# Batch 1 of a mixer-and-FFN kernel: rows split in SBUF and transposed by the DMA queue instead of by TensorE

## What is computed

```python
x = x + layernorm(attn(layernorm(x)))
x = x + layernorm(ffn(layernorm(x)))

# attn: i, f, g = x @ Wi.T, x @ Wf.T, x @ Wg.T          (512 x 512 weights)
gate = sigmoid(f);  v = silu(i) * (1 - gate)
_, o = associative_scan(combine, (gate, v), axis=1)     # o[t] = gate[t]*o[t-1] + v[t]
o = o * rsqrt(mean(o*o) + EPS) * gnorm_w * g * sigmoid(g);  return o @ Wo

# ffn: hidden = silu(x @ W1.T) * (x @ W3.T)             (hidden width 2048)
hidden = fwht(hidden);  return hidden @ W2.T
```

## Time and profile before

| | |
|---|---|
| median of 3 runs | 684.47 us (682.37 to 684.54) |
| the profiled execution | 685.5 us, its span 683.7 us |
| PE busy | 659.0 us, 96% |
| DVE busy | 413.2 us, 60% |
| ACT busy | 352.6 us, 52% |
| POOL busy | 237.7 us, 35% |
| DMA | 114.12 MB, mean 167 GB/s |

### The profile page before, as it was taken

One profiled execution on the slowest core, in us unless ns is written; L12 is line 12 of the kernel. 1 busy time (PEld: TensorE's weight loads), 2 busy tenths in 40 slices (PEclk: granted clock), 3 DMA queues, 4 the chain that ended last, 5 costly groups with the idle time before them and its releaser, 6 DMA issues. The chain is left out here.

```text
span 683.7 us, 11532 instructions
## 1 busy us (share of the span) xinstructions
PE 659.0 (96%) x4332; PEld 427.1 (62%) x4332; DVE 413.2 (60%) x791; ACT 352.6 (52%) x633; POOL 237.7 (35%) x216
## 2 busy tenths in 40 slices
PE   4998999999999899999999999999999999999996
PEld 2444444444456667776776777677777777777762
DVE  5889999999999999976459203144212113621224
ACT  5999886373674767645346334344333343533231
POOL 1328368574762145165227112112211111411121
PEclk9999999999999999999999999999999999999999
DMA  8992453107245465984796225568334233752002
GB/s 324 408 403 101 108 140 59 46 21 170 92 157 184 169 202 191 319 291 171 177 308 238 110 108 178 106 199 289 137 131 165 83 133 108 243 204 81 29 1 92
DMA packets 60743, 114.12 MB, mean 167 GB/s; under 512 B 40464, under 2 KB 40720, under 8 KB 56080
## 3 DMA queue, kind: packets, MB, share of 16 engines
q1 hardware_dynamic: 60688, 113.39, 49.8%
HBM read 80.87 MB, written 23.07 MB: 152 GB/s over the span
## 5 line engine op out<-in xcount | busy, mean ns | idle before, releaser
L646 PE MATMUL ps<-xb,ring 128*128 128x256 f16 (+1 forms) x696 | 209.5, 301 | 5.5 <-ACT ps L990 3.0
L648 PE MATMUL ps<-xb,ring 128*128 128x256 f16 (+1 forms) x696 | 209.4, 301 | 0.0
L647 PE MATMUL ps<-xb,ring 128*128 128x256 f16 (+1 forms) x696 | 209.4, 301 | 0.0
L1451 POOL TENSOR_TENSOR ring<-sga,ring 128x512 f16<-128x512 f32 x64 | 80.1, 1256 | 289.5 <-ACT ring L1036 289.4
L646 PE MATMUL ps<-ring 128*128 128x256 f16 x384 | 104.8, 273 | 0.0
L647 PE MATMUL ps<-ring 128*128 128x256 f16 x384 | 104.7, 273 | 0.0
L648 PE MATMUL ps<-ring 128*128 128x256 f16 x384 | 104.7, 273 | 0.0
L646 PE MATMUL ps<-w2t,ring 128*128 128x512 f16 x256 | 97.1, 379 | 1.1 <-ACT ring L921 1.1
L647 PE MATMUL ps<-w2t,ring 128*128 128x512 f16 x256 | 97.1, 379 | 0.0
L648 PE MATMUL ps<-w2t,ring 128*128 128x512 f16 x256 | 97.1, 379 | 0.0
L646 PEld LDWEIGHTS ps<-xb,ring 128*128 128x128 f16 x696 | 68.1, 98 | 43.0 <-ACT ps L990 5.2
(11 more groups left out here) (169 smaller groups left out, 1053.1 us busy)
## 6 DMA issues: line engine op xcount, KB each, us to landing
ring<-w_comb SPq DMA_DIRECT2D x24, 1792.0 KB, 7.5
...
```

The source lines that it names most:

```text
L646: pe.matmul(dst, a_hi, b_hi, start=start, stop=False, skip_group_check=onto)
L647: pe.matmul(dst, a_hi, b_lo, start=False, stop=False, skip_group_check=onto)
L648: return pe.matmul(dst, a_lo, b_hi, start=False, stop=stop, skip_group_check=onto)
L1451: pool.tensor_tensor(hid(b, c, 1), sga[:, c % 2], hid(b, c, 0), ALU.subtract).then_inc(hid_lo, 1)
```

## The change

`AHEAD` goes from 2 to 1, so batch 1 takes the second form: `XT.1.0` to `XT.1.3` leave TensorE's order, `XD.1.0` to `XD.1.3` enter SP's, and ACT and DVE do `XT.1.*` from `rows` in SBUF into `sga` and `hsp`. Since batch 2 uses the same two buffers, `XT.2.*` on ACT now waits for batch 1's DMA transposes. `XL.2.t` waits for `XT.1.t`'s low part on DVE instead of for TensorE's transpose. All five tables are new (banks too).

```diff
-AHEAD = 2
+AHEAD = 1
...
                 elif b > 1:
-                    sp.wait_ge(xt_mm if b == 2 else xt_lo, TC * (b - 1) + t + 1)
+                    sp.wait_ge(xt_lo, TC * (b - 1) + t + 1)
                 sp.dma_start(rows[:, t], x_rows[TC * b + t]).then_inc(ld_x[t], 16)
...
             def transpose_x(b, t):
                 sp.wait_ge(xt_lo, TC * b + t + 1)
-                if t == 0:
+                if t == 0 and b > 1:
                     for read in (f_mm, i_mm, g_mm):
                         sp.wait_ge(read, KC * (b - 1))
...
                     act.wait_ge(aw_norm, 3)
-                    if b == 3:
-                        act.wait_ge(ld_xt, 16 * TC)
+                    if b > AHEAD:
+                        act.wait_ge(ld_xt, 16 * TC * (b - AHEAD))
                     act.activation(parts_of_x(t)[:, 0], rows[:, t], ACT.Copy).then_inc(xt_hi, 1)
```

The places of the tables that the prediction speaks of:

```diff
 PE:   (banks left out)
-... AN.3.0 XT.1.0 F.0.2 XT.1.1 F.0.3 I.0.0 I.0.1 I.0.2 XT.1.2 G.0.0 G.0.1 G.0.2 I.0.3 G.0.3 XT.1.3 H2.0.0 H2.0.1 F.1.0
+... AN.3.0 F.0.2 F.0.3 I.0.0 I.0.1 I.0.2 G.0.0 G.0.1 G.0.2 I.0.3 G.0.3 H2.0.0 H2.0.1 F.1.0
 SP:
-... UL.6.0 UL.7.0 XL.2.0 NL.5.0 XL.2.1 NL.6.0 XL.2.2 NL.7.0 XL.2.3 XD.2.0 XL.3.0 ...
+... UL.6.0 UL.7.0 NL.5.0 XL.2.0 XD.1.0 XL.2.1 XL.2.2 NL.6.0 NL.7.0 XD.1.1 XD.1.2 XL.2.3 XD.1.3 XD.2.0 XL.3.0 ...
 POOL:
-... FW.0.5 FW.0.6 X1.2.0 P.0.0 FW.0.7 S.0.1 ...
+... FW.0.5 P.0.0 FW.0.6 FW.0.7 X1.2.0 S.0.1 ...
 DVE:
-... XT.2.0 FD.1.4 MS.0.0 FD.1.5 FD.1.6 FD.1.7 Y.0.0 X1.3.0 FD.2.0 XT.2.1 YN.0.0 XT.2.2 S.1.0 Y.0.1 ...
+... XT.2.0 FD.1.4 FD.1.5 FD.1.6 MS.0.0 FD.1.7 XT.2.1 FD.2.0 X1.3.0 Y.0.0 XT.2.2 S.1.0 YN.0.0 Y.0.1 ...
```

More of the change, by code:

```diff
@@ new lines @@
+F.2.0:4 G.1.3:3 I.2.0:1 G.2.0:2 F.2.1:5 H2.1.0:6 H2.1.1:4 H2.2.0:0 H2.2.1:3 MS.1.0:7 Y.1.0:1 Y.1.1:2 Y.1.2:5 Y.1.3:6
+I.2.1:4 G.2.1:0 F.2.2:3 I.2.2:7 H2.3.0:1 H2.3.1:2 G.2.2:5 F.2.3:6 I.2.3:4 F.3.0:0 G.2.3:3 I.3.0:7 G.3.0:5 MS.2.0:1
+Y.2.0:6 Y.2.1:2 H2.4.0:0 Y.2.2:4 H2.4.1:3 Y.2.3:7 F.3.1:5 I.3.1:1 G.3.1:6 F.3.2:0 H2.5.0:3 H2.5.1:2 I.3.2:5 G.3.2:4
+F.3.3:7 I.3.3:0 GP.0.0:6 G.3.3:1 H2.6.0:3 GP.0.1:7 GQ.0.0:5 GQ.0.1:4 GR.0.0 H2.6.1:2 GR.0.1 MS.3.0:0 Y.3.0:1 Y.3.1:3
+GP.0.2:6 GU.0.0 GU.0.1 H2.7.0:2 GP.0.3:7 Y.3.2:0 H2.7.1:1 GQ.0.2:5 Y.3.3:3 GR.0.2 GQ.0.3:4 GU.0.2 GP.0.4:6 GR.0.3
@@ new lines @@
+D.0.0 GU.0.3 D.0.1 GQ.0.4:5 D.0.2 GR.0.4 GP.0.5:7 D.0.3 D.0.4 D.0.5 D.0.6 D.0.7 GQ.0.5:4 GU.0.4 GR.0.5 D.0.8 GP.0.6:6
+D.0.9 D.0.10 D.0.11 GU.0.5 GP.0.7:7 GQ.0.6:5 D.0.12 D.0.13 D.0.14 D.0.15 GR.0.6 GQ.0.7:4 D.0.16 D.0.17 GR.0.7 GU.0.6
+D.0.18 D.0.19 GU.0.7 GP.0.8:6 D.0.20 D.0.21 GQ.0.8:5 GP.0.9:7 D.0.22 D.0.23 GR.0.8 GQ.0.9:4 D.0.24 D.0.25 D.0.26
+GR.0.9 D.0.27 GP.0.10:6 GU.0.8 D.0.28 D.0.29 GU.0.9 GP.0.11:7 D.0.30 D.0.31 GQ.0.10:5 GQ.0.11:4 GR.0.10 GR.0.11
+GU.0.10 D.0.32 D.0.33 D.0.34 GP.0.12:6 D.0.35 D.0.36 D.0.37 D.0.38 GQ.0.12:5 GU.0.11 D.0.39 GP.0.13:7 GR.0.12
@@ new lines @@
+GQ.0.13:4 GU.0.12 GR.0.13 GP.0.14:6 D.0.40 D.0.41 GU.0.13 D.0.42 D.0.43 D.0.44 D.0.45 GQ.0.14:5 D.0.46 GP.0.15:7
+GR.0.14 GQ.0.15:4 D.0.47 GP.1.0:6 GR.0.15 D.0.48 D.0.49 D.0.50 GU.0.14 D.0.51 D.0.52 D.0.53 GP.1.1:7 D.0.54 GQ.1.0:5
+D.0.55 GU.0.15 GR.1.0 GU.1.0 GP.1.2:6 D.0.56 D.0.57 GQ.1.1:4 D.0.58 GR.1.1 D.0.59 D.0.60 D.0.61 GQ.1.2:5 D.0.62 GU.1.1
+GP.1.3:7 GR.1.2 D.0.63 GU.1.2 GP.1.4:6 D.1.0 GQ.1.3:4 GQ.1.4:5 GR.1.3 D.1.1 D.1.2 D.1.3 GP.1.5:7 GU.1.3 GR.1.4 D.1.4
+D.1.5 GQ.1.5:4 GP.1.6:6 GU.1.4 D.1.6 GR.1.5 D.1.7 GQ.1.6:5 GP.1.7:7 D.1.8 D.1.9 D.1.10 GR.1.6 GU.1.5 D.1.11 D.1.12
@@ new lines @@
+GP.1.8:6 D.1.13 D.1.14 D.1.15 GQ.1.7:4 D.1.16 GR.1.7 D.1.17 GU.1.6 D.1.18 D.1.19 D.1.20 GP.1.9:7 GU.1.7 D.1.21
+GQ.1.8:5 D.1.22 GQ.1.9:4 GR.1.8 GU.1.8 D.1.23 D.1.24 GR.1.9 GP.1.10:6 GP.1.11:7 D.1.25 GQ.1.10:5 D.1.26 GR.1.10 GU.1.9
+GP.1.12:6 GU.1.10 D.1.27 D.1.28 D.1.29 D.1.30 D.1.31 D.1.32 D.1.33 GQ.1.11:4 GQ.1.12:5 GR.1.11 GU.1.11 GR.1.12
+GP.1.13:7 GU.1.12 D.1.34 D.1.35 D.1.36 D.1.37 D.1.38 D.1.39 GQ.1.13:4 D.1.40 GR.1.13 GU.1.13 GP.1.14:6 GP.1.15:7
+GQ.1.14:5 GQ.1.15:4 GR.1.14 D.1.41 GR.1.15 D.1.42 D.1.43 D.1.44 D.1.45 D.1.46 D.1.47 GU.1.14 GU.1.15 D.1.48 GP.2.0:6
@@ new lines @@
+GP.2.1:7 D.1.49 D.1.50 D.1.51 GQ.2.0:5 D.1.52 D.1.53 D.1.54 D.1.55 D.1.56 GR.2.0 D.1.57 D.1.58 D.1.59 GP.2.2:6 GU.2.0
+GQ.2.1:4 D.1.60 D.1.61 GR.2.1 D.1.62 D.1.63 GU.2.1 GQ.2.2:5 GP.2.3:7 GR.2.2 GQ.2.3:4 GU.2.2 GR.2.3 GP.2.4:6 GP.2.5:7
+GU.2.3 GQ.2.4:5 D.2.0 GR.2.4 GQ.2.5:4 D.2.1 GR.2.5 GU.2.4 GP.2.6:6 GU.2.5 D.2.2 GP.2.7:7 GQ.2.6:5 D.2.3 D.2.4 D.2.5
+GQ.2.7:4 D.2.6 GR.2.6 D.2.7 GR.2.7 D.2.8 GU.2.6 D.2.9 GP.2.8:6 D.2.10 GU.2.7 D.2.11 GP.2.9:7 D.2.12 GQ.2.8:5 D.2.13
+GR.2.8 D.2.14 D.2.15 GQ.2.9:4 D.2.16 GU.2.8 D.2.17 GR.2.9 GP.2.10:6 GU.2.9 D.2.18 D.2.19 GQ.2.10:5 GP.2.11:7 GR.2.10
@@ new lines @@
+GQ.2.11:4 GP.2.12:6 D.2.20 D.2.21 D.2.22 D.2.23 D.2.24 D.2.25 GU.2.10 GR.2.11 GU.2.11 GQ.2.12:5 GP.2.13:7 GR.2.12
+GQ.2.13:4 GP.2.14:6 GU.2.12 D.2.26 D.2.27 D.2.28 D.2.29 D.2.30 D.2.31 D.2.32 D.2.33 D.2.34 GQ.2.14:5 D.2.35 D.2.36
+GR.2.13 D.2.37 D.2.38 GP.2.15:7 GR.2.14 D.2.39 GU.2.13 D.2.40 D.2.41 D.2.42 D.2.43 GQ.2.15:4 GP.3.0:6 D.2.44 GU.2.14
+GR.2.15 D.2.45 GU.2.15 GQ.3.0:5 D.2.46 GR.3.0 GU.3.0 GP.3.1:7 D.2.47 GP.3.2:6 GQ.3.1:4 GQ.3.2:5 GR.3.1 D.2.48 D.2.49
+GR.3.2 D.2.50 D.2.51 GU.3.1 GU.3.2 D.2.52 GP.3.3:7 D.2.53 D.2.54 GQ.3.3:4 D.2.55 GP.3.4:6 D.2.56 GR.3.3 D.2.57
@@ new lines @@
+GQ.3.4:5 D.2.58 D.2.59 GR.3.4 D.2.60 GU.3.3 GP.3.5:7 D.2.61 GU.3.4 GQ.3.5:4 D.2.62 D.2.63 D.3.0 D.3.1 GR.3.5 D.3.2
+GP.3.6:6 D.3.3 D.3.4 D.3.5 GU.3.5 GQ.3.6:5 GP.3.7:7 GR.3.6 GQ.3.7:4 D.3.6 GR.3.7 D.3.7 GU.3.6 D.3.8 GU.3.7 D.3.9
+D.3.10 D.3.11 D.3.12 GP.3.8:6 D.3.13 D.3.14 GQ.3.8:5 D.3.15 GR.3.8 D.3.16 GP.3.9:7 D.3.17 GP.3.10:6 GQ.3.9:4 GU.3.8
+GR.3.9 D.3.18 D.3.19 GQ.3.10:5 GP.3.11:7 GR.3.10 D.3.20 D.3.21 GU.3.9 GU.3.10 D.3.22 D.3.23 GP.3.12:6 GQ.3.11:4
+GQ.3.12:5 GR.3.11 GR.3.12 GU.3.11 GP.3.13:7 D.3.24 D.3.25 D.3.26 D.3.27 D.3.28 D.3.29 D.3.30 D.3.31 GQ.3.13:4
@@ L81 @@
+GP.3.14:6 D.3.32 D.3.33 GU.3.12 GR.3.13 D.3.34 GQ.3.14:5 GP.3.15:7 GU.3.13 D.3.35 GR.3.14 D.3.36 GU.3.14 D.3.37 D.3.38
+D.3.39 GQ.3.15:4 D.3.40 GR.3.15 GU.3.15 D.3.41 D.3.42 D.3.43 D.3.44 D.3.45 D.3.46 D.3.47 D.3.48 D.3.52 D.3.56 D.3.60
+D.3.49 D.3.53 D.3.57 D.3.61 D.3.50 D.3.54 D.3.58 D.3.62 D.3.51 D.3.55 D.3.59 D.3.63
 """
@@ L99 @@
[L99 to L103, removed]
+F.3.2 H2.5.0 H2.5.1 S.3.1 I.3.2 P.3.1 G.3.2 S.3.2 F.3.3 WT.4.0 I.3.3 WT.4.1 SH.1.0 P.3.2 GP.0.0 WT.5.0 WT.5.1 G.3.3
@@ new lines @@
+GP.0.1 GQ.0.0 S.3.3 GQ.0.1 P.3.3 H2.6.0 GA.0.0 H2.6.1 UP.0.0 GA.0.1 WT.6.0 GP.0.2 YN.3.0 WT.6.1 WT.7.0 WT.7.1 SH.2.0
+YN.3.1 H2.7.0 GP.0.3 UP.0.1 H2.7.1 GQ.0.2 YN.3.2 GA.0.2 GQ.0.3 GA.0.3 GP.0.4 WT.8.0 WT.8.1 WT.9.0 WT.9.1 GQ.0.4 SH.3.0
+YN.3.3 UP.0.2 ZT.1.0 UP.0.3 ZT.1.1 GP.0.5 GQ.0.5 GA.0.4 GA.0.5 GP.0.6 SH.4.0 UP.0.4 UP.0.5 GP.0.7 WT.10.0 GQ.0.6
+WT.10.1 WT.11.0 WT.11.1 ZT.1.2 GQ.0.7 ZT.1.3 ZT.1.4 ZT.1.5 GA.0.6 GA.0.7 WT.12.0 WT.12.1 GP.0.8 WT.13.0 ZT.1.6 SH.5.0
+UP.0.6 GQ.0.8 UP.0.7 WT.13.1 GP.0.9 GQ.0.9 GA.0.8 GA.0.9 SH.6.0 UP.0.8 UP.0.9 GP.0.10 GP.0.11 WT.14.0 GQ.0.10 WT.14.1
@@ L122 @@
[L122 to L125 removed]
+X1.2.1 S.0.2 X2.2.0 P.0.2 FD.1.0 XT.1.3 FD.1.1 S.0.3 X1.2.2 P.0.3 X1.2.3 X2.2.1 FD.1.2 X2.2.2 X2.2.3 FD.1.3 XT.2.0
@@ new lines @@
+GU.0.10 WT.15.0 GR.0.11 WT.15.1 GU.0.11 SA.7.0 UP.0.10 SO.7.0 UP.0.11 Z1.2.0 GR.0.12 Z1.2.1 Z1.2.2 GU.0.12 GR.0.13
+GU.0.13 UP.0.12 Z1.2.3 Z2.2.0 Z2.2.1 Z2.2.2 Z2.2.3 ZT.2.0 UP.0.13 ZT.2.1 ZT.2.2 GR.0.14 GU.0.14 ZT.2.3 ZT.2.4 ZT.2.5
+GR.0.15 GU.0.15 ZT.2.6 UP.0.14 UP.0.15 GR.1.0 GU.1.0 GR.1.1 GU.1.1 UP.1.0 V.0.0 V.0.1 W.0.0 V.0.2 UP.1.1 W.0.1 GR.1.2
+GU.1.2 V.0.3 W.0.2 GR.1.3 GU.1.3 UP.1.2 W.0.3 UP.1.3 Z1.3.0 GR.1.4 Z1.3.1 GU.1.4 Z2.3.0 Z2.3.1 Z1.3.2 ZT.3.0 ZT.3.1
+Z2.3.2 GR.1.5 GU.1.5 UP.1.4 Z1.3.3 Z2.3.3 ZT.3.2 GR.1.6 ZT.3.3 GU.1.6 ZT.3.4 UP.1.5 ZT.3.5 ZT.3.6 GR.1.7 GU.1.7 UP.1.6
```

163 lines of the change are left out of this document (59 added, 104 removed).

## The result

The changed kernel takes 689.23 us (median of 4 runs, 688.71 to 690.01) against 683.85 for the kernel before beside it: ratio 1.0083, 95% interval 1.006 to 1.0105. The forecast was 687.4 us, slower. The profiled execution took 688.79 us, span 687.0. Single executions of the same early orders also begin up to 1.7 us apart, so of a start only differences above that mean something.

A forecast was written before the change was run, and what follows sets the result against it. Bound: PE and DVE both full from 60 to 285 us (221.0 and 217.6 of 225), then PE alone. Sum: 685.5 + 2.9 = 688.4, and 687.4 us as the runs' median lies 1.0 below the profiled execution; range 683.0 to 690.0.

The forecast's parts named there:

- 1.7 us off TensorE are worth 0: Ahead of H2.0.0: four transposes leave PE, 1.7 us, but become idle time since F.1.0 is not ready; gain 0.
- F.1.0 at 63.5, +3.9: Start of batch 1: F.1.0 waits for the last DMA transpose, XD.1.3, and starts 3.9 us later (3.4 to 5.3).
- No slack: ACT from 28 to 58 us: busy 29.78 of 30.00 us, so it can't reach XT.1.3 earlier than 58.23 us.
- The queue, 0: DMA queue before F.1.0: dry at 59.4 us, just before XD.1.3 is issued; 0, at most 2 us more.
- The clock, +2.1: After PE's 5.7 us idle before F.1.0: PE restarts at 1.2 GHz, costing 2.1 us (0 to 2.6).
- DVE, +2.8 behind XT.2.1: DVE near 72 to 77 us: three steps now come behind XT.2.1, 2.8 us of work left (0 to 3.5).
- F.1.1 at 84.7 without a wait: PE at F.1.1: Y.0.3 ends 6.0 us late at 84.7, no wait for S.1.0; 5.0 us behind the old 79.77.
- Back to 2.9 at 285 us, then carried: PE up to 285 us: lateness shrinks from 5.0 to about DVE's 2.8, taken as 2.9, then carried to the end.
- Rival 1: 60 to 285 us: DVE's 2.8 us do not reach PE, lateness is absorbed; 684.5 us, up to 686.4; chance 0.28.
- five places: 60 to 285 us: PE waits on DVE and ACT at only five places, 3.9 us in all; argument for Rival 1.
- The later tables, 0, at most 1.5 to lose: From 285 us on: new orders change neighbours of about the same steps; 0, with 2.4 us to gain, 1.5 to lose.
- the cushion: PE's waits up to 285 us, which in Rival 1 absorb its lateness: 3.9 - 3.9 = 0.

The follow-up runs named there:

- e10: Changed kernel with SP's and DVE's border orders of before, plus early steps moved on ACT, DVE, SP and POOL for an earlier F.1.0 and fewer DVE waits; 683.8 us.
- e12: e10 with one more step moved: P.2.3 ahead of ZT.0.6 in DVE's order; 682.8 us.
- e11: e2 with SP's and DVE's border steps as in the kernel before; 687.0 us.
- e2: Kernel before, its transposes unchanged, with the changed kernel's late orders on all five engines (PE from D.0.0 on); 689.0 us.
- e4: Changed kernel with 12 matmuls of no use ahead of H2.0.0 and 26 ahead of F.1.0 to keep TensorE busy; 688.8 us.
- e8: Changed kernel with the late orders of before, and XT.1.3 (ACT, DVE) and XD.1.1 to XD.1.3 (SP) moved earlier; 690.1 us.
- e6: Changed kernel with SP's seventeen steps at the border near 362 us in the order of the kernel before; 686.6 us.

## Why the prediction came out, step by step

- **1.7 us off TensorE are worth 0.** Right: PE waits 2.85 us at H2.0.0 and 5.75 at F.1.0. That they would be worth something with F.1.0 free fits e10 and e12, but no run isolates it: these two differ from the kernel before in much else.
- **F.1.0 at 63.5, +3.9.** Measured 62.27, +2.64. The mechanism is right, the term was too large because ACT reached XT.1.3 at 56.52 and not at 58.2. Most of that is the late execution of before: in e11 and e2, with the early orders of before, ACT gets there at 57.20 and 57.26 us, and in the kernels with the new early part that leave XT.1.3 in its place between 55.82 and 57.34. "No slack" held, but it said nothing of where ACT's list starts. Against e11 F.1.0 is 3.66 late, close to the forecast. SP issued XD.1.3 at 58.60, 0.4 us behind XL.2.3 as forecast; to F.1.0 it took 3.7 us, forecast 3.6.
- **The queue, 0.** Right at this place, but the transposes cost SP time: see below.
- **The clock, +2.1.** Measured 1.7 (9.49 against 7.77 us from F.1.0 to MS.0.0; e4). It fell already in H2.0.0, which took 2.39 in place of 1.96 us. The Trainium skill (TensorE: Matmul & The Clock Gate, "What's actually happening") calls the throttled state the default; the trace now agrees inside the kernel, at 0.50. But removing the fall gives 0.4 us at the end (e4), within the spread of the runs: its price was hidden, and what hid it is in the next point.
- **DVE, +2.8 behind XT.2.1.** The wait came (1.43) and DVE lost 2.4 us between the scans at 60.5 and 79.8, but more of it through X1.2.3's root (1.71 us of idle time), a chain over ACT and POOL that I hadn't followed. And Y.2.0 came between 163.2 and 164.2 us in every kernel with the new early orders but e10 and e12, wherever F.1.1 was (82.0 to 84.2 us). Where F.1.1 came at 82.9 us or later the wait in front of Y.2.0 was 0.3 to 0.8 us, where it came earlier (e4, e8) 1.7 and 2.4: there DVE's place for P.2.3 is the second stop. No step of the forecast named it.
- **F.1.1 at 84.7 without a wait.** Measured 82.92, without a wait. It is 1.8 us less late than forecast, 1.3 from F.1.0's start and 0.4 from the clock. Against e11's 78.75 it is 4.2 late, where the forecast had 5.0.
- **Back to 2.9 at 285 us, then carried.** The waits shrank from 2.96 to 0.96 us up to 285 us, so 1.15 was left there and not 2.9; one wait of 0.21 at 302 us makes it 1.35 at 345. About 1.0 of the missing 1.75 is again the late execution of before. (Rival 1's "five places" where PE waits on DVE and ACT are four on ACT and one of 0.31 us on issue; PE waits for DVE nowhere there before.)
- **The later tables, 0, at most 1.5 to lose.** This step failed. In the profile they cost 1.75 us from 345 us on (0.54 of waits and 1.7 of clock at the border, less 0.49 at 471 us), and SP's steps alone 2.6 in the timed runs (e6). I had looked for it in the order around PE's waits; it lay in SP's list, where a 256 KB store had moved behind a weight load.

So the near hit, 687.4 for 689.2, is in good part luck. In the profiles two errors of opposite sign cancel, 1.5 too much early and 1.75 too little late. Of the 1.8 us between 687.4 and 689.2, 0.4 is the profiled execution of after against the 688.4 of the sum, 0.44 is its distance below its own median, and 1.0 is what the forecast took off because the profiled execution of before lay above its median. Median against median the loss was 5.4 us, nearly twice the 2.9 of the forecast, and the sums above account for 3.1 of it; 1.0 more is the late execution of before, and the rest is not explained by any trace. Rival 1 asked for F.1.0 before 63.6 us and at full rate. The first was met and the second not; the cushion took 1.8 of the 3.15 us and didn't hold.
